# Moving the look at the feed-forward weights' low bits from VectorE to ScalarE, in a decoder layer on one core

## The reference, cut to what matters

```
x = layernorm(x + attention(x))            # causal, rotary positions, 16 heads
x = layernorm(x + cross_attention(x, ctx)) # 77 keys
h = silu(x @ w1.T * s1) * (x @ w2.T * s2)  # 256 -> 1024
h = gelu(h @ h1.T * s_h1)                  # 1024 -> 1024
h = gelu(h @ h2.T * s_h2)
x = layernorm(x + h @ w3.T * s3)           # 1024 -> 256
```

## Time and profile before

| | before |
|---|---|
| median of 3 runs | 966.22 us (963.57 to 967.8) |
| the profiled execution | 965.38 us |
| its span on the core | 963.7 us |
| TensorE's mean granted clock | 0.958 of full speed |
| busy: PE, PE weight load | 878.7 us, 576.5 us |
| busy: DVE, ACT, POOL | 535.0 us, 354.5 us, 328.0 us |
| DRAM copies of the weights | issued at 12.2 to 14.1 us, landed 10.2 to 35.9 us later |
| the three loads of pieces | issued at 71.7 to 72.8 us |
| the 22 ORs on DVE | 182.0 to 226.9 us |

### The profile page before, as it was taken

How to read it: one execution, slowest core, us unless ns; L and a number is a source line. 1 busy time by engine, 2 the same in 40 slices (tenths; PEclk the granted TensorE clock), 3 DMA queues, 4 the chain that set the end, 5 groups by cost and what they waited for, 6 DMA issues and landing times.

```text
span 963.7 us, 14216 instructions
## 1 busy us (share of the span) xinstructions
PE 878.7 (91%) x5034; PEld 576.5 (60%) x5034; DVE 535.0 (56%) x1385; ACT 354.5 (37%) x746; POOL 328.0 (34%) x554
## 2 busy tenths in 40 slices
PE   5879999898999999988989899998999999999996
PEld 2544444235666667876666654443476667887885
DVE  4697888677666633145343588883366653116113
ACT  0315766464433411114111166766733342122210
POOL 4412323447300444425222233233440024335332
PEclk9867999879999999999999999998999999999998
DMA  9909101002200232325222024340000000000000
GB/s 328 311 1 387 74 2 46 23 0 76 88 1 1 68 95 102 110 75 166 88 88 88 29 94 164 133 155 2 1 2 1 2 1 1 1 1 23 1 1 23
DMA packets 23849, 68.71 MB, mean 71 GB/s; under 512 B 4401, under 2 KB 11569, under 8 KB 23601
## 3 DMA queue, kind: packets, MB, share of 16 engines
q1 hardware_dynamic: 23776, 67.77, 20.1%
HBM read 65.40 MB, written 13.63 MB: 82 GB/s over the span
## 4 chain that ended last, share of the span: by engine, by line
PE 74%; DVE 14%; POOL 4%; issue 4%; ACT 2%; SPq 1%; DMA 0%; POOLq 0%; DVEq 0%; ACTq 0%
PE bank L833 23%; PE bank L643 6%; PE bank L661 6%; PE bank L612 6%; PE bank L821 4%; DVE max_raw L1131 4%; PE bank L742 4%; DVE bank L1133 4%; PE bank L752 4%; PE bank L830 3%; PE bank L693 3%; PE bank L598 2%; PE bank L556 2%; PE bank L763 2%; POOL prob_s L1398 2%
## 5 line engine op out<-in xcount | busy, mean ns | idle before, releaser
L964 ACT ACTIVATE prob_s<-bank 128x512 f32<-128x512 f32 (+3 forms) x384 | 163.5, 497 | 91.8 <-PE bank L643 91.5
L1427 POOL TENSOR_TENSOR hid_lo_s<-act_raw_s,hid_hi_s 128x512 fp32r<-128x512 f32 x96 | 123.7, 1288 | 212.2 <-DVE hid_hi_s L1294 177.4
L612 PE MATMUL bank<-k_t_s,q_t_s 64*128 64x512 f32 (+3 forms) x384 | 138.4, 451 | 25.7 <-DVE max_raw L1133 16.4
L1398 POOL TENSOR_SCALAR_AFFINE_SELECT prob_s<-prob_s 128x128 f32<-128x128 f32 x256 | 83.1, 341 | 161.1 <-ACT prob_s L964 158.8
L1294 DVE CAST hid_hi_s<-act_raw_s 128x512 fp32r<-128x512 f32 x64 | 30.5, 477 | 193.1 <-ACT act_raw_s L1025 192.8
L1133 DVE CUSTOM_DVE_ANT_0 bank<-bank,causal_bf 128x128 f32<-128x128 f32 (+3 forms) x256 | 122.8, 509 | 15.2 <-PE bank L612 13.1
L643 PE MATMUL bank<-q_t_s,k_t_s 64*128 64x512 f32 (+3 forms) x384 | 115.7, 416 | 2.0 <-issue 1.2
L1025 ACT ACTIVATE act_raw_s<-bank,scales 128x512 f32<-128x512 f32 x64 | 43.7, 689 | 180.8 <-PE bank L833 180.8
L612 PEld LDWEIGHTS bank<-k_t_s,q_t_s 64*128 64x128 f32 x384 | 63.5, 199 | 70.3 <-DVE max_raw L1133 31.3
L643 PEld LDWEIGHTS bank<-q_t_s,k_t_s 64*128 64x128 f32 x384 | 59.1, 199 | 76.6 <-ACT prob_s L964 50.4
L1131 DVE TENSOR_REDUCE max_raw<-bank 128x1 f32<-128x512 f32 x128 | 82.3, 684 | 36.0 <-PE bank L612 36.0
(11 more groups left out here) (154 smaller groups left out, 1511.5 us busy)
## 6 DMA issues: line engine op xcount, KB each, us to landing
ring_s<-scratch SPq DMA_DIRECT2D x34, 512.0 KB, 3.2
home_s<-scratch SPq DMA_DIRECT2D x22, 512.0 KB, 6.0
checked_s<-scratch SPq DMA_DIRECT2D x3, 3584.0 KB, 21.3
ring_moved_s<-scratch SPq DMA_DIRECT2D x10, 512.0 KB, 3.2
x_t_s<-in_x_t SPq DMA_DIRECT2D x2, 1024.0 KB, 5.2
x_tok_s<-in_x SPq DMA_DIRECT2D x2, 1024.0 KB, 7.5
out<-tok SPq DMA_DIRECT2D x16, 128.0 KB, 1.7
q_t_s<-max_rows SPq DMA_DIRECT2D x64, 4.0 KB
```

What stands on the lines that cost most here:

```text
L612: mm(out[:, 0:k1 - k0], qkt(q, p, 0)[r, P * qt:P * (qt + 1)], qkt(q, p, 1)[r, k0:k1], start=True, stop=True).then_inc(S["max_mm"], 1)
L964: act.activation(prob[q][4 * (s % 2) + j][:, 0:n], S_BANK[j][:, 0:n], ACT.Exp, scale=SCALE).then_inc(S["exp_done"], 1)
L1398: pool.affine_select(out=pr, in_=pr, compare_op=ALU.is_ge, fill=0.0, base=0, pattern=[[1, P]], channel_multiplier=-1).then_inc(S["select_d ...
L1427: pt(dst[1][:, m], act_raw[q][r % 3][:], dst[0][:, m].bitcast(F32), ALU.subtract).then_inc(S["f_lo"], 1)
```

## The change

The look is made on ScalarE, and earlier:

- SP loads the 22 pieces straight from `w_ffn` into `checked` at the start, in three parts of 7, 7 and 8 pieces, in the place of the four DRAM copies.
- ACT makes one `ACTIVATE` (Copy) for each piece, at steps -19 to 2. It reads the low 16 bits of each word as unsigned integers, writes them as bfloat16 to a tile that nobody reads (`low_halves`) and adds them up into `low_sums[:, n]`. Each waits for the one before.
- At step 48 DVE takes the maximum of the 22 sums of each partition and limits it to 1.
- The DRAM copies `w_ffn` to `scratch` are issued in five parts, behind the row moves of steps 3, 9, 15, 21 and 27.
- ACT, POOL and SP wait for the 22 sums, PE for the two small operations of DVE. POOL no longer clears `low_bits`.

```
+CHECK_PARTS = ((0, 7), (7, 14), (14, PIECES))
+SCRATCH_PARTS = ((0, 5), (5, 10), (10, 14), (14, 18), (18, PIECES))
-def check_steps(n):
-    first = max_step(NP - 1, NU - 1) + 1
-    return first + n * (LAST - first) // PIECES
+def check_step(n):
+    return FIRST_STEP + 1 + n
...
 # SP
-        for i, j in ((0, 4), (4, 12), (12, 20), (20, PIECES)):
-            sp.dma_start(a["scratch"][i:j], a["w_ffn"][i:j]).then_inc(L["scratch_in"], 16)
+        for part, (i, j) in enumerate(CHECK_PARTS):
+            sp.dma_start(checked[:, i:j], a["w_ffn"][i:j].rearrange("i p n -> p i n")).then_inc(L["check_in"][part], 16)
         for s in range(FIRST_STEP, S_END):
-            if s == rows_step(2):
-                sp.wait_ge(L["scratch_in"], 16 * 4)
-                for i in range(0, PIECES - 1, 7):
-                    sp.dma_start(checked[:, i:i + 7], a["scratch"][i:i + 7].rearrange("i p n -> p i n")).then_inc(L["check_in"], 16)
             attention(0, s)
-        sp.wait_ge(S["check_op"], 2)
-        sp.dma_start(checked[:, 0], a["scratch"][PIECES - 1]).then_inc(L["check_last_in"], 16)
-        sp.wait_ge(S["check_op"], PIECES + 3)
+            for n, (i, j) in enumerate(SCRATCH_PARTS):
+                if s == rows_step(2 + n):
+                    sp.dma_start(a["scratch"][i:j], a["w_ffn"][i:j]).then_inc(L["scratch_in"], 16)
+        sp.wait_ge(S["check_act"], PIECES)
+        sp.wait_ge(L["scratch_in"], 16 * len(SCRATCH_PARTS))
 # PE
-        pe.wait_ge(S["check_op"], PIECES + 3)
+        pe.wait_ge(S["check_op"], 2)
 # ACT
+        def check_piece(n):
+            for part, (i, j) in enumerate(CHECK_PARTS):
+                if n == i:
+                    act.wait_ge(L["check_in"][part], 16)
+            if n:
+                act.wait_ge(S["check_act"], n)
+            act.activation(low_halves[:], checked[:, n].bitcast(U16)[:, ::2], ACT.Copy, accum_out=low_sums[:, n:n + 1]).then_inc(S["check_act"], 1)
 # ACT, in attention(q, s), behind the exponentials and evacuations of the step
+            for n in range(PIECES):
+                if q == 0 and check_step(n) == s:
+                    check_piece(n)
 # DVE
-            tt(low_bits[:], low_bits[:], checked[:, n % (PIECES - 1)].bitcast(U32), ALU.bitwise_or).then_inc(S["check_op"], 1)
 # DVE, step LAST = 48
-                dve.tensor_scalar(low_bits[:], low_bits[:], LOWBITS, None, ALU.bitwise_and).then_inc(S["check_op"], 1)
-                dve.tensor_reduce(low_max[:], low_bits[:], AXX, ALU.max).then_inc(S["check_op"], 1)
+                dve.tensor_reduce(low_max[:], low_sums[:], AXX, ALU.max).then_inc(S["check_op"], 1)
+                dve.tensor_scalar(low_max[:], low_max[:], 1.0, None, ALU.min).then_inc(S["check_op"], 1)
 # POOL
-        pool.memset(low_bits[:], 0).then_inc(S["check_op"], 1)
-        pool.wait_ge(S["check_op"], PIECES + 3)
+        pool.wait_ge(S["check_act"], PIECES)
```

More of the change, by code:

```diff
@@ L24 @@
 U8 = mybir.dt.uint8
-U32 = mybir.dt.uint32
+U16 = mybir.dt.uint16
 I32 = mybir.dt.int32
@@ L50 @@
 QKBUF = 5
-LOWBITS = 0xFFF
 PIECES = 22
@@ L275, in decoder_layer @@
         vx = sb("vx", [P, VROW], F32)
+        low_sums = sb("low_sums", [P, PIECES], F32)
         low_max = sb("low_max", [P, 1], F32)
@@ L335, in decoder_layer @@
         xmask_u8 = at(0, "xmask_u8", [P, NT, CTX], U8, O_T)
-        checked = at(1, "checked", [P, PIECES - 1, PW], F32, 0)
-        low_bits = at(1, "low_bits", [P, PW], U32, ARENA - 4096)
+        checked = at(1, "checked", [P, PIECES, PW], F32, 0)
+        low_halves = at(1, "low_halves", [P, PW], BF16, 4096 * PIECES)
         hid = [[[at(q, f"hid{b}_{n}", [P, KH, CHUNK], F32R, 25600 + 32768 * b + 16384 * i)
@@ L357, in decoder_layer @@
         w_in, mask_in, scratch_in = sem("w_in"), sem("mask_in"), sem("scratch_in")
-        w_qkv_in, rope_in, check_in, check_last_in = sem("w_qkv_in"), sem("rope_in"), sem("check_in"), sem("check_last_in")
+        w_qkv_in, rope_in, check_in = sem("w_qkv_in"), sem("rope_in"), [sem(f"check_in{i}") for i in range(len(CHECK_PARTS))]
         ring_in = [sem(f"ring_in{i}") for i in range(RING)]
@@ L363, in decoder_layer @@
         S = {n: sem(n) for n in PER}
-        for n in "check_op flag_mm flag_set".split():
+        for n in "check_act check_op flag_mm flag_set".split():
             S[n] = sem(n)
@@ L368, in decoder_layer @@
             a=a, act_raw=act_raw, bank=bank, bias_v=bias_v, bias_o=bias_o, bk_t=bk_t, blocks=blocks, bq_t=bq_t, causal_bf=causal_bf,
-            check_in=check_in, check_last_in=check_last_in, checked=checked, cos_t=cos_t, ctx_t=ctx_t, hid=hid, home=home,
-            home_in=home_in, ident=ident, ident_bf=ident_bf, kx_blocks=kx_blocks, kx_f=kx_f, kx_hl=kx_hl, no_key=no_key, low_any=low_any, low_bits=low_bits,
+            check_in=check_in, checked=checked, cos_t=cos_t, ctx_t=ctx_t, hid=hid, home=home,
+            home_in=home_in, ident=ident, ident_bf=ident_bf, kx_blocks=kx_blocks, kx_f=kx_f, kx_hl=kx_hl, no_key=no_key, low_any=low_any, low_halves=low_halves, low_sums=low_sums,
             low_max=low_max, mask_in=mask_in, max_raw=max_raw, max_rows=max_rows, max_split=max_split, mean_var=mean_var,
@@ L393, in build_layer @@
     stats, mean_var, var_eps, rstd = L["stats"], L["mean_var"], L["var_eps"], L["rstd"]
-    low_bits, low_max, low_any, checked = L["low_bits"], L["low_max"], L["low_any"], L["checked"]
+    low_halves, low_sums, low_max, low_any, checked = (L[k] for k in ("low_halves", "low_sums", "low_max", "low_any", "checked"))
     w_in, out_done, set_pool, set_dve = L["w_in"], L["out_done"], L["set_pool"], L["set_dve"]
@@ L1056, in _ @@
             attention(0, s)
-        act.wait_ge(S["check_op"], PIECES + 3)
+        act.wait_ge(S["check_act"], PIECES)
         for s in range(FFN_STEP):
@@ L1314, in attention @@
                     split_max(q, p)
-            for n in range(PIECES):
-                if q == 0 and check_steps(n) == s:
-                    check_piece(n)
             for n in range(2 * NG):
@@ L1323, in attention @@
             if q == 0 and s == LAST:
-                dve.wait_ge(S["check_op"], PIECES + 1)
-                dve.tensor_scalar(low_bits[:], low_bits[:], LOWBITS, None, ALU.bitwise_and).then_inc(S["check_op"], 1)
-                dve.wait_ge(S["check_op"], PIECES + 2)
-                dve.tensor_reduce(low_max[:], low_bits[:], AXX, ALU.max).then_inc(S["check_op"], 1)
+                dve.wait_ge(S["check_act"], PIECES)
+                dve.tensor_reduce(low_max[:], low_sums[:], AXX, ALU.max).then_inc(S["check_op"], 1)
+                dve.wait_ge(S["check_op"], 1)
+                dve.tensor_scalar(low_max[:], low_max[:], 1.0, None, ALU.min).then_inc(S["check_op"], 1)
             norm_work(q, "S", s)
```

6 lines of the change are left out of this document (removed).

## The result

The changed kernel takes 956.49 us (median of 4 runs, 952.70 to 960.31), the kernel before 966.41 us beside it (963.57 to 967.80). The ratio is 0.9866, with a 95% interval of 0.9822 to 0.9909: faster by 1.3%. The prediction was 958.7 us, 0.8% less than before. Its direction is right; the ratio stands for 0.9866 x 966.22 = 953.3 us, a little outside the range of 954 to 964.5.

A forecast was written before the change was run, and what follows sets the result against it. TensorE, busy for 91% of the span, was taken as the bound. Terms -11.76 (tail), +0.3 (step 48), +3.4 (first turns) and +0.5 (steps -13 to 2, clock) gave -7.5 us: 958.7 us against the median 966.22, range 954 to 964.5.

The forecast's parts named there:

- 3C - 0.33: Three checks between pair 0's four evacuations delay the first maximum unit by 3.4 us (bounds 2.5 and 6.4).
- its good case: All goes well: a look costs 0.95 us and the tail has full clock; -11.2 us in all, 955.0 us.
- tail, with step 48: Sequence 0's tail shrinks by 11.76 us to sequence 1's length; step 48's small operations add 0.3 (bounds 0 and 1.9).
- steps -13 to 2, clock: Checks 19 to 21 behind steps 0 to 2's exponentials, and PE's clock, add 0.5 us (bounds 0 and 2).
- from there to pair 7: The stretch from pair 2's split to pair 7's has no term in the sum; 0 us.
- C = 1.25 us: One look on ACT: 1.02 for columns, 0.03 SBUF source, 0.14 accumulator read, 0.05 wait; bounds 0.95 and 2.25 us.
- as measured, whatever the mechanism: The tail's gain is the two sequences' difference, 53.09 - 41.33 = 11.76 us, without settling its cause; bounds 9.4 and 14.0.
- DMA at nothing: Direct loads land in time for the checks, and the DRAM copies in parts cost and gain nothing.
- Rival 1: ACT becomes the bound of the head, eating the tail's gain at C of 2.05, 970.5 us at 2.25; chance 0.06.
- 16 + 22C: Rival 1's sum: ACT's time from 38.4 us to step 3, other work plus 22 checks, against 49.7 us available.
- Rival 2: The look's DVE work was hidden anyway, so only the head's 3.9 us remain: 970 us; chance 0.03.
- Rival 3: Gain partly eaten by C of 1.5, a late clock rise and a slow tail: -3 us, 963.2 us; chance 0.17.

The follow-up runs named there:

- experiment 2: The changed kernel without the 22 ACTIVATEs, sums set to 0, so no look at the weights; 954.02 us, ratio 0.9843 to the kernel before.
- experiment 5: The changed kernel with ACT's looks moved into its gaps, none between pair 0's four evacuations; 957.51 us, ratio 0.9884 to the kernel before.
- experiment 3: The changed kernel's DMA order alone, with the old look on DVE (two-operand ORs at steps 33 to 47, mask and maximum at 48); 971.75 us, ratio 1.0008.
- experiment 4: The changed kernel with the look on DVE at steps 33 to 47 as one-operand maxima over low halves; 955.32 us, ratio 0.9878 to the kernel before.
- experiment 1: The changed kernel measured again without an edit; 957.88 us, ratio 0.990 to the kernel before.
- experiment 8: Old two-operand look on DVE with the new DMA order, step 48's mask and maximum over 22 words only; 967.40 us in one run, no ratio.
- experiment 9: The changed kernel a third time, without an edit; 961.40 us, ratio 0.9913 to the kernel before.
- The repeats: The changed kernel measured twice more without an edit; 957.88 us (ratio 0.990) and 961.40 us (ratio 0.9913) to the kernel before.
- Experiment 7: The changed kernel with each look on ACT made twice, 44 ACTIVATEs; 970.73 us, ratio 1.0008 to the kernel before.

## Where the prediction was right and where it failed

The mechanism was the predicted one, term by term; sizes failed, and they made the gain too small. Three steps did it. The price of the look at the first turns, 3C - 0.33, was put at 3.4 us and measured 2.64. The stretch from the split of pair 2 to pair 7 was put at nothing and gave 1.12 us by the clock. And the range allowed "about a microsecond" for scatter beyond its good case, to a kernel whose untouched part alone varies by 10 us.

| term | predicted | profiled execution |
|---|---|---|
| tail, with step 48 | -11.76 + 0.3 = -11.46 | -12.03 |
| first turns | +3.4 | +2.64 |
| steps -13 to 2, clock | +0.5 | +0.68 |
| from there to pair 7 | 0 | -1.12 |
| to the cross-attention's start | -7.5 | -9.83 |

**Of the terms in the sum, 3C - 0.33 at the first turns was mis-sized most, by C = 1.25 us.** The ACTIVATE's own time was well estimated (1.02 + 0.03 predicted, 1.05 measured). I then added the accumulator's read and a wait for the predecessor in full; in the chain both overlap with the evacuation behind, and C is 1.03, near my lower bound of 0.95. Back to back, where a look follows a look, it is some 1.2 (starts at 43.33, 44.52 and 45.70 us). Experiments 2 and 5 confirm where the price lies: without the looks, or with them behind the fourth evacuation, the first unit is at 40.72 and 41.33.

**The tail** became sequence 1's, as the sum had it, within 0.3 us. The 0.3 us for step 48 did not appear: the maximum over 22 columns takes 167 ns, and PE's wait behind it is 0.2 us, as in sequence 1. In nine executions without ORs sequence 0's tail took 38.99 to 41.25 us: some 39.0 at a clock of 1.00 (39.30 with the reductions), 40.5 at 0.96, 41.1 to 41.25 at 0.92. These are gains of 11.8 to 14.1 us, and my bounds were 9.4 and 14.0. The reason that the sum did not rest on is shown by experiments 3 and 4. Taking the two tails' difference "as measured, whatever the mechanism" gave the right number, but hid that the work could have stayed on DVE.

**Pair 7's 1.12 us** is clock, and luck: the same instructions between the splits of pairs 6 and 7 took 18.66 us in the kernel after, about 19.8 before and in experiment 1, and 21.8 in experiments 2, 3, 8 and 9. The prediction says that PE's waits set off a fall of the clock. In this stretch the traces don't show it: PE waited for 2.1 us in the kernel after, at 1.00, and for 1.4 us in experiment 9, the same kernel, at 0.77.

**DMA at nothing** held. The three loads landed 13.6, 22.1 and 32.2 us after their issue, against 11.9, 21.3 and 29.5 that I had carried over, in time for every check. Experiment 3 shows that the new order neither helps nor hurts by more than 0.4%. It doesn't hold the earlier loads of sequence 1; that these gave nothing is seen only in that the stretch from the first to the second cross-attention product, 467.17 us before, is no shorter in any of the three traces of the changed kernel (471.96, 468.93 and 469.34).

**The remainder.** The chain's -9.83 us and the medians' difference of -9.92 us agree, but by luck in part, since the two profiled executions differ by only 5.1 us at their ends. The repeats' medians differ by 11.4 and 8.6 us. The -12.9 us that the first ratio stands for is further than any of these, and its interval runs from -8.8 to -17.2 us. So by the chain the forecast's effect was short by some 2.3 us, 1.3 of them in the two terms above and 1.1 in the clock of pair 7's stretch. The other 3 us of the first ratio are in no trace; the repeats don't have them and lie inside the range, so most likely they are scatter of four executions against four. That is what the range's microsecond for scatter left no room for.

**The rivals.** Rival 1, ACT as the bound, was ruled out at C = 1.03 to 1.2. Experiment 7 tests its sum with a doubled look, which is C = 2.2 (evacuations 2.71 us apart, less 0.49). By 16 + 22C that is 64.4 us; measured are 60.8, from 38.43 to the split of pair 2 at 99.26. Only 21 of the 22 doubled looks lie ahead of that split, and ACT's other work there is 15.1 us (in the kernel before) and not 16, which gives 61.3. So the mechanism of this rival was right and its price some 3 us too high at that mark, and what it foretold as level with before, a head 11.4 us longer, is what experiment 7 has (99.26 against 87.83, ratio 1.0008). Rival 2, DVE's work hidden anyway, was false for this look and true for another one: in experiment 4 nearly as much DVE work is hidden. Rival 3 did not come: the repeats (0.990 and 0.9913 stand for 956.6 and 957.8 us) lie on the other side of the forecast's 958.7 from its 963.2.

## What to carry to other kernels

When one engine's idle-time work slows another, change the form of the instruction before changing its engine: here a reduction with one SBUF operand, at the same place and of the same length, gave the whole gain. Test the form, for one operand alone did not free POOL beside the casts. Two stages of one trace with the same instructions, with and without the suspect, give the size of an effect; only a run that keeps the occupancy and changes the form gives its cause. Put a filler on an in-order engine behind the last instruction that something waits for, not between its predecessors, and leave room for the clock when an effect of 1% is to be forecast.

## What the runs showed of the hardware

- An ACTIVATE with a sum is two instructions in the trace: 1.05 us for 1024 16-bit halves read at a step of two halves (the slope of plain copies of 32-bit words, 388 and 599 ns for 256 and 512 columns, gives the same), and an accumulator read of 0.19 us. The two together hold up a following evacuation by 1.03 us, and a following look by some 1.2.
- One select gets through per two-input OR (1.27 us each, four in 5.08 us), against 0.29 us alone or beside the reductions (1208 ns), which are not longer for it: the maximum over 1024 words took 1220 ns with no select beside it. A cast from SBUF to SBUF, with one input, makes the select beside it 0.39 to 0.57 us long.
- TensorE's granted clock varies between executions of the same instructions with little difference in PE's waits: in two traces of the changed kernel 18.66 us at 1.00 (waits of 2.1 us) and 21.80 us at 0.77 (waits of 1.4 us) for the stretch from pair 6 to pair 7. What decides it between two executions stays open.
